# Graph kernel: one-hot comparisons that read the row of numbers from PSUM, and VectorE in place of ScalarE in the second layer

## What the kernel computes

```python
x = x + L0(h)   # m = h[src] + edge_attr_96;         segment_sum(m, dst); two-layer MLP
x = x + L1(h)   # m = relu(h[src] + edge_attr_32 @ We + be); segment_sum(m, dst); MLP, batch norm
x = x + L2(h)   # three graph convolutions: segment_sum(norm * hw[row], col)
x = x + L3(h)   # three attention layers:
    e   = leaky_relu(alpha_s[src] + alpha_d[dst], 0.2)
    ex  = exp(e - segment_max(e, dst)[dst])
    out = segment_sum(h[src] * (ex / den[dst])[:, :, None], dst)
```

## Time and profile before

| what | value |
|---|---|
| time, median of 3 runs | 12916.29 us (12902.06 to 12917.15) |
| the profiled execution's own time | 12913.76 us |
| its span (first to last instruction) | 12911.9 us |
| busy: POOL | 8319.3 us (64%) |
| busy: PE, PEld | 6375.1 us (49%), 5484.1 us (42%) |
| busy: DVE | 5751.3 us (45%) |
| busy: ACT | 1887.1 us (15%) |

### The profile page before, as it was taken

The page is one execution under the profiler, slowest core; times in us unless marked ns, Lnnn a source line. Parts: engine busy times, 40 slices in busy tenths (PEclk is TensorE's granted clock), DMA queues, the critical chain, the costliest instruction groups (busy, mean ns, idle before and its releaser), DMA issues.

```text
span 12911.9 us, 134309 instructions
## 1 busy us (share of the span) xinstructions
PE 6375.1 (49%) x36085; PEld 5484.1 (42%) x36085; DVE 5751.3 (45%) x16150; ACT 1887.1 (15%) x4810; POOL 8319.3 (64%) x8396
## 2 busy tenths in 40 slices
PE   0198821455555559995444444444444443444443
PEld 0188611234444447774333333333333343333333
DVE  8455300133222341224555555555555564555555
ACT  0199300044444430000000000000000000000000
POOL 1877777467777730002777777577777757777775
PEclk8555765766666659997555555555555555555555
DMA  8144511122222207663222222222222222222222
GB/s 271 23 103 103 145 48 40 53 56 54 53 53 53 53 17 238 213 211 115 64 64 64 65 64 64 53 64 64 64 65 64 64 55 62 64 64 66 64 64 56
DMA packets 1052968, 1038.36 MB, mean 80 GB/s; under 512 B 641834, under 2 KB 758358, under 8 KB 1052336
## 3 DMA queue, kind: packets, MB, share of 16 engines
q1 hardware_dynamic: 704544, 611.05, 16.3%
q0 software_dynamic: 264160, 337.47, 12.9%
q10 hardware_dynamic: 83664, 82.78, 2.0%
HBM read 935.74 MB, written 96.55 MB: 80 GB/s over the span
## 4 chain that ended last, share of the span: by engine, by line
POOL 59%; issue 21%; PE 11%; DVE 5%; ACTq 2%; DMA 1%; DVEq 1%; ACT 0%; POOLq 0%; SPq 0%; PEldq 0%
POOL sb_HG L565 46%; POOL edge_counts L626 13%; PE sums L958 3%; ACTq L651 2%; DVE sb_ACC L1938 1%; PE psA L958 1%; PE psB L958 1%; PE sums L895 1%; PE psC L958 1%; PE psD L958 1%; DMA sb_HG<-attention_table,sb_NOW 1%; PE psA L843 1%; PE psD L853 0%; PE psD L877 0%; PE psC L853 0%
## 5 line engine op out<-in xcount | busy, mean ns | idle before, releaser
L565 POOL DMA_INDIRECT sb_HG<-attention_table,sb_NOW x4992 | 5070.1, 1016 | 1571.8 <-issue 1490.5
L895 PE MATMUL sums<-sb_HG 128*128 128x100 f32 x9984 | 2078.1, 400 | 447.5 <-issue 439.6
L895 PEld LDWEIGHTS sums<-sb_HG 128*128 128x128 f32 x9984 | 2045.3, 314 | 457.5 <-issue 457.5
L626 POOL DMA_INDIRECT edge_counts<-sb_HG x1625 | 1631.1, 1004 | 765.3 <-issue 495.0
L565 POOL DMA_INDIRECT sb_HG<-feature_table,sb_NOW x1612 | 1522.2, 944 | 556.3 <-issue 490.8
L1938 DVE TENSOR_TENSOR sb_ACC<-sb_ACC,sums 128x100 f32 x4992 | 1273.7, 255 | 933.3 <-PE sums L895 357.9
L905 PEld LDWEIGHTS sums<-sb_HG 128*128 128x128 f32 x6656 | 1325.6, 300 | 314.9 <-issue 314.7
L905 PE MATMUL sums<-sb_HG 128*128 x6656 | 1341.6, 385 | 143.3 <-ACT sb_HG L695 72.1
L1477 DVE TENSOR_TENSOR sb_ACC<-sb_ACC,sums 128x97 f32 (+1 forms) x3328 | 848.7, 255 | 605.9 <-PE sums L905 136.6
L1071 PE MATMUL psD<-sb_ident,sb_SB 128*128 128x128 f32 x156 | 74.1, 475 | 2099.1 <-DVE sb_SB L1819 2099.1
L760 ACT ACTIVATE psC<-sb_SB 128x128 f32<-128x128 f32 x156 | 43.8, 281 | 6590.8 <-DVE sb_SB L1891 6590.8
(11 more groups left out here) (443 smaller groups left out, 9052.2 us busy)
## 6 DMA issues: line engine op xcount, KB each, us to landing
sb_HG<-edge_counts SPq DMA_DIRECT2D x1152, 256.0 KB, 3.3
sb_H<-rel_rows SPq DMA_DIRECT2D x312, 512.0 KB, 3.8
sb_HG<-attention_table,sb_NOW POOLq DMA_INDIRECT x4992
sb_HG<-in_edge_attr_dram SPq DMA_DIRECT2D x201, 384.0 KB, 3.5
edge_counts<-sb_LW ACTq DMA_DIRECT2D x12, 6272.0 KB, 42.5
edge_counts<-sb_HG POOLq DMA_INDIRECT x1625
sb_HG<-feature_table,sb_NOW POOLq DMA_INDIRECT x1612, 2.5
sb_EA<-in_edge_attr_dram SPq DMA_DIRECT2D x201, 128.0 KB
```

The costliest lines, as they stand in the source:

```text
L565: pool.indirect_dma_start(to, None, rows, bass.IndirectOffsetOnAxis(ap=index, axis=0)).then_inc(landed, 16)
L626: pool.indirect_dma_start(every_count, bass.IndirectOffsetOnAxis(ap=slot_of[:, f:f + 1], axis=0), tally[:, f:f + 1], None).then_inc(scatte ...
L895: last = nc.tensor.matmul(bank[:, k // 4, k % 4 * width:(k % 4 + 1) * width], HOT[:, hot, k, :], G[:, slot, k, 0:width], start=True, stop= ...
```

## The change

The changed kernel builds all these one-hots on VectorE and takes the row of numbers from PSUM. `hots` gets the row as an argument. In the second layer the row is copied once to `psD[:, 0:P]`, and VectorE makes the one-hots of one group at a time in `HOT`; ScalarE's `hot_of`, the second `REL_neg` and its `rel_ready` are gone there (`load_rows` counts one less). In attention it is copied to `psC[:, P:2 * P]` ahead of each layer; ScalarE's exponents lie in the first 128 columns of that bank. The first layer keeps `hot_of`. Line numbers in the changed kernel are 4 lower from line 743 to 1634, 5 lower for the former lines 1639 to 1649, and the same again from line 1770 on.

```diff
-                sp.wait_ge(rel_ready, 3 + l)
+                sp.wait_ge(rel_ready, 2 + l)
...
-                if hots:
-                    hot_of(t, 1 - half, U * g + U, g + 1, 2, place=1)
...
-            act.wait_ge(rel_ready, 2)
             lift_attrs(0, t.base["ea_flipped"] + 1)
-            hot_of(t, 0, 0, 0, 2, place=1)
-            for g in range(GROUPS):
-                turn(g, g % 2, g % RING1, g + 1 < LOADS, g + 1 < GROUPS, g < LOADS)
+            for g in range(LOADS):
+                turn(g, g % 2, g % RING1, g + 1 < LOADS)
...
-            def hots(slot, k, groups):
+            def hots(numbers, slot, k, groups):
                 n = U * groups
                 return v.tensor_tensor(HOT[:, slot:slot + groups, :, :].rearrange("p s k n -> p (s k) n"),
-                                       iota_row[:, :].unsqueeze(1).broadcast_to([P, n, P]),
+                                       numbers.unsqueeze(1).broadcast_to([P, n, P]),
                                        REL[:, ds(k, n)].unsqueeze(2).broadcast_to([P, n, P]), ALU.is_equal)
...
-            v.tensor_scalar(REL_neg[1], REL[:, 0:TILES], -1.0, None, ALU.mult).then_inc(rel_ready, 1)
...
             add_product(0, 0, 0, 0)
+            link(v.tensor_copy(psD[:, 0:P], iota_row[:, :]))
+            hots(psD[:, 0:P], 0, 0, 1).then_inc(SEM["hot_built"], 1)
             for g in range(GROUPS):
+                if g + 1 < GROUPS:
+                    hots(psD[:, 0:P], (g + 1) % 2, U * g + U, 1).then_inc(SEM["hot_built"], 1)
                 if g + 1 < LOADS:
                     add_product(g + 1, (g + 1) // SIX, (g + 1) % SIX, (g + 1) % RING1)
...
                 link(v.memset(lone[:, :], -BIG))
+                link(v.tensor_copy(psC[:, P:2 * P], iota_row[:, :]))
...
-                    hots(n % 8, 8 * U * it + U * n, 2).then_inc(SEM["hot_built"], 2)
+                    hots(psC[:, P:2 * P], n % 8, 8 * U * it + U * n, 2).then_inc(SEM["hot_built"], 2)
```

More of the change, by code:

```diff
@@ L730, in relu, with turn @@
                 nc.scalar.activation(rows, rows, ACT.Relu).then_inc(SEM["rows_ready"], 1)
-            def turn(g, half, slot, lifts=True, hots=True, relus=True):
+            def turn(g, half, slot, lifts=True, relus=True):
                 if lifts:
                     lift_attrs(half + 1, g + (t.base["ea_flipped"] + 2))
-                if hots:
-                    hot_of(t, 1 - half, U * g + U, g + 1, 2, place=1)
                 if relus:
                     relu(slot, 2 * g + (t.base["summed"] + 2))
-            act.wait_ge(rel_ready, 2)
             lift_attrs(0, t.base["ea_flipped"] + 1)
-            hot_of(t, 0, 0, 0, 2, place=1)
-            for g in range(GROUPS):
-                turn(g, g % 2, g % RING1, g + 1 < LOADS, g + 1 < GROUPS, g < LOADS)
+            for g in range(LOADS):
+                turn(g, g % 2, g % RING1, g + 1 < LOADS)
             lift_mlp(Stage("L1mlp"), 1, 2)
```

## The result

The changed kernel takes 12588.85 us (median of 4 runs, 12565.95 to 12590.25), the kernel before 12909.17 (4 runs). The ratio is 0.9749, 95% interval 0.9732 to 0.9765: 2.5% faster. 12600 was predicted. The profiled execution has a span of 12588.0 us against 12911.9. One execution among the experiments, of the one called attention alone, was slow: it took 12951.88 us at a granted clock of 0.563 where the others had 0.63, and it is left out of that kernel's time and ratio.

A forecast was written before the change was run, and what follows sets the result against it. POOL's gathers, count times duration, were taken to bound the kernel. From 12913.8 us, -340 (holds gone) + 29 (holds returned) - 3 (second layer) = -314 gave 12600 us, range 12550 to 12660.

The forecast's parts named there:

- The bound: Attention and second layer: POOL's gather count times gather duration sets the length, with pauses of about 0.3 us.
- The hold: Attention: line 1467, with two SBUF inputs, holds gathers at their 0.12 us point; removing this gains 340 us.
- the bounds 324 and 359: Attention's gain: from below 306 holds x 1.06 = 324 us, from above 72 ns excess x 4992 gathers = 359.
- The returned part: Attention: line 1805 behind the first comparison newly holds a gather, 0.19 us x 153 batches = 29 us back.
- The comparison's time: VectorE: the 2048-element comparison keeps its time with a PSUM row; 1024 elements take 1.22 us.
- The second layer: Gather stretch stays at 2013 us; start -1, end about -2, in all -3 us.
- -5.21 and +2.6: Second layer's end: TensorE's 5.21 us wait for ScalarE goes; six last groups at VectorE's 4.25 us add 2.6.
- A: Rival: which input is in SBUF decides, attention stays, second layer gets 202 holds; 12943 us, towards 13130; 7%.
- B: Rival: slots come free too late, POOL waits for TensorE and VectorE, half the gain; about 12750 us; 3%.
- C: Rival: the holds have another cause that stays, such as writing the result; no change, 12914 us; 3%.

The follow-up runs named there:

- attention alone: Kernel before, with only the attention comparisons reading the row from PSUM and the second layer keeping ScalarE's one-hots: 12587.8 us, ratio 0.9759.
- one comparison of two: Changed kernel, with the second of the two attention comparisons of a batch reading its row from SBUF again: 12741.0 us (one run).
- the sixth experiment: Changed kernel, with line 1805 made a tensor_tensor without fast mode, its column of numbers in PSUM: 12564.17 us (5 runs), beside 12573.32 for the changed kernel.
- The exchanged inputs: Changed kernel, with REL (SBUF) as first input and the row (PSUM) as second in attention's comparison: 12589.52 us (one run).
- the third experiment: Changed kernel, with the second layer's VectorE comparisons reading the row of numbers from SBUF: 12640.56 us (one run).

## Why the prediction was right

**The bound.** POOL's count of gathers times their duration set the length: right, by the windows and by the waits of 0.3 us at most.

**The hold.** A gather held at its 0.12 us point until the comparison ends: right, and the case's largest term. Of the bounds 324 and 359 I took 340. Summing what each gather takes above 0.945 us, where its point lies inside line 1467, gives 340.4 us over 306 gathers in the kernel before, and 0 in the changed one. The bounds were worked out, the point between them was not, so a fit to 0.4 us is luck: a hold is 1.11 us on average, where the two in the rows gave 1.06. That the gather reads its row numbers at that moment is an inference; no run shows what it does there, only when it can be held and by which instructions. The experiment with one comparison of two gives the price a second time, 1.02 us for each.

**The returned part.** 0.19 us behind each first comparison, 29 us, was forecast. The mechanism and the place were right, and the size was the term that was mis-sized: where the point lies inside the line 1805 behind the first comparison, it is 20.9 us over 145 gathers of the changed kernel, 0.14 each, and nothing in the kernel before. In the second profile of the changed kernel it is 15.7 us over 147. The other holds by line 1805 were there already, 10.0 us in the kernel before, most of them at a batch's first one, and they stay at about 8. Together line 1805 goes from 10 to 29 us. With all holds counted, attention lost 322.6 us where 311 were forecast, and with the 2 to 3 us of the second layer that is the 12588 in place of 12600. The rule of the Trainium skill on two-port modes (SBUF — State Buffer, "Who interferes with whom") is borne out by the sixth experiment, which takes the mode away and the hold with it.

**The comparison's time** stayed, and the 1.22 us forecast for 1024 elements was measured at 1224 ns.

**The second layer.** -1 at the start: the first gather begins 0.9 us earlier. At the end, from the last gather's end to the end of the additions, 38.7 us became 36.9, where -2 was written (the terms written down, -5.21 and +2.6, give -2.6); six last groups at 4.25 us were measured at 4.2. The stretch between is 2013.1 and 2012.7 us.

**Rivals.** A falls with the result itself: it wanted gathers of about 2 us beside line 1463 and lengthened ones in the second layer, and both stayed at 0.94. The exchanged inputs add that the other order holds nothing either. B falls with POOL's waits; even 2.7 us more VectorE work per batch, in the sixth experiment, did not call it up. C, and with it the inference in the same section of the Trainium skill that a tensor_tensor does not stall the making of descriptors, fall with the result and with the third experiment, where the same instruction costs 49 us from SBUF and nothing from PSUM.

Two sizes in the experiments were off as well: 36 us for 49 in the third, because the moment at which a comparison begins was taken from one group; and 28 for 20 in the sixth, because line 1805 held only 24 us in the profile beside it, and because other short instructions came into the point's way. All of these sizes depend on phase, which moves from one profile of the same kernel to the next.

## What to carry to other kernels

Where POOL issues gathers back to back and sets the pace, look at the distribution of their durations, not the mean: here a second peak near 2 us told that something holds them, and the ends of the two timelines, a constant 0.82 us apart, told which instruction. Then try one input of the long VectorE instructions in PSUM, which cost nothing in their own time here (2283 for 2286 ns). Cutting them in two also helped, as a gather slips in between, but it gave only a little over half of the gain (12714 us, between 12893 and 12573). Moving 678 us of work off ScalarE was worth nothing here, since POOL did not wait for ScalarE, and with the row in SBUF that move would have cost 49 us.

## What the runs showed of the hardware

- A VectorE instruction with two SBUF inputs delayed a gather here by way of one moment, 0.12 us after the gather's start, and the gather ended 0.82 us after that instruction. An instruction that began 0.15 us or less before the moment came too late to hold it, and one that began 0.18 us or more before it held it every time (173 and 96 gathers in the kernel with halves). I had not expected so sharp an edge, and it makes a size depend on hundredths of a microsecond of phase.
- The size of a hold is what is left of the instruction at that moment, and not its length. The comparisons of 2.28 us cost 1.11 us each in the kernel before (340.4 us for 306), those of 1.22 us in the second layer 0.24 (49 us for 200), but the second halves of the same 1.22 us cost 1.02, because they had only just begun.
- Line 1805, a tensor_scalar in bf16 from SBUF to SBUF, meets the gather at a later moment too, and there the gather can also hold VectorE. In the timeline of the changed kernel below, the second of two such instructions runs over the later part of the gather and ends at 7837.70, and the gather ends at 7837.81, 0.12 us behind it (0.11 by the rounded rows); so do all 16 gathers of this trace in which an instruction of line 1805 started 0.38 to 0.48 us after the gather. In the second pair line 1805 starts 0.49 us into the gather, which keeps its 0.94 us, and it takes 0.70 us instead of 0.48. In this trace 54 of them started 0.48 to 0.59 us into a gather, and all ended 1.19 to 1.20 us after its start. Such late holds of gathers came to 1.2 us in all here. The comparisons of line 1467 with two SBUF inputs do not hold a gather there: 278 of them in the kernel before began in a gather's first 0.48 us and ran past its end, and 275 of those gathers kept their 0.94 or 0.95 us.

```profile
7836.74 1.07 POOL L565 DMA_INDIRECT sb_HG<-attention_table,sb_NOW  x1 [0.30 <-PE sums L891]
7836.82 0.88 DVE L1805 TENSOR_SCALAR sb_EA<-sb_H,sb_iota_col 128x1024 bf16<-128x1024 bf16 x2
...
6205.99 0.94 POOL L565 DMA_INDIRECT sb_HG<-attention_table,sb_NOW  x1 [0.30 <-issue]
6206.48 0.70 DVE L1805 TENSOR_SCALAR sb_EA<-sb_H,sb_iota_col 128x1024 bf16<-128x1024 bf16 x1
```

- A tensor_tensor of 1024 bf16 elements with one input in f32 from PSUM took 1214 ns, the tensor_scalar from SBUF most often 0.48 us. Beside POOL the slower one was the better choice, by 19.6 us of 6266 in the stretches of attention.
